# Transposing ctx of a second batch with VectorE's 32x32 blocks in an fp32 cross-attention and FFN kernel

## The reference, cut to what matters

```python
x = x + xattn(layernorm(x), ctx)      # x, ctx: (8, 256, 1024)
x = x + ffn(layernorm(x))             # 4-bit weights, 1024 x 1024

def xattn(text, features):
    Q = text @ Wq.T + bq
    K = features @ Wk.T + bk
    attn = softmax(Q @ K.T / sqrt(1024))
    return attn @ features
```

## Time and profile before

| | us |
|---|---|
| median of 3 runs | 547.48 |
| the profiled execution, its own time | 547.35 |
| its span, first to last instruction | 545.6 |
| TensorE busy | 539.3 (99%) |
| VectorE busy | 372.4 (68%) |
| ScalarE busy | 268.0 (49%) |
| GpSimd busy | 187.2 (34%) |

### The profile page before, as it was taken

One profiled execution on the slowest core, in us unless ns is written; L12 is line 12 of the kernel. 1 busy time (PEld: TensorE's weight loads), 2 busy tenths in 40 slices (PEclk: granted clock), 3 DMA queues, 4 the chain that ended last, 5 costly groups with the idle time before them and its releaser, 6 DMA issues.

```text
span 545.6 us, 7455 instructions
## 1 busy us (share of the span) xinstructions
PE 539.3 (99%) x2686; PEld 452.0 (83%) x2686; DVE 372.4 (68%) x616; ACT 268.0 (49%) x474; POOL 187.2 (34%) x147
## 2 busy tenths in 40 slices
PE   8999999999999999999999999999999999999997
PEld 7888888887777877778898999998788888888886
DVE  4989775787698774793424555574768779778742
ACT  6983444414767582343437766686563243324210
POOL 1072000010011000000326877777756644753530
PEclk9999999999999999999999999999999999999999
DMA  8942100359688756836384899898346775774311
GB/s 270 314 157 79 38 1 0 123 156 313 195 228 292 204 193 193 262 86 192 126 293 144 298 362 355 321 389 346 144 123 244 220 216 203 230 232 134 98 77 77
DMA packets 56036, 108.14 MB, mean 198 GB/s; under 512 B 12000, under 2 KB 32552, under 8 KB 53824
## 3 DMA queue, kind: packets, MB, share of 16 engines
q1 hardware_dynamic: 49472, 101.38, 54.1%
q10 hardware_dynamic: 6528, 6.29, 5.7%
HBM read 67.74 MB, written 39.85 MB: 197 GB/s over the span
## 4 chain that ended last, share of the span: by engine, by line
PE 86%; DVE 4%; ACT 3%; DMA 3%; issue 1%; POOL 1%; ACTq 0%; SPq 0%; DVEq 0%; POOLq 0%
PE bank L1337 22%; PE bank L1339 22%; PE bank L1338 22%; PE bank L1384 5%; PE bank L1390 5%; PE bank L1387 5%; PE bank L1438 2%; DMA xq<-xn_scratch 1%; ACT yin L868 1%; POOL cn_lo L578 1%; DVE xq L1035 1%; DMA wq_stage<-in_L_xattn_Wq 1%; DVE xT_lo L932 1%; PE bank L1347 1%; ACT cn_hi L627 1%
## 5 line engine op out<-in xcount | busy, mean ns | idle before, releaser
L1337 PE MATMUL bank<-xT_hi,m_hi 128*128 128x512 f32 x256 | 101.0, 395 | 0.0
L1339 PE MATMUL bank<-xT_hi,m_lo 128*128 128x512 f32 x256 | 99.7, 390 | 0.0
L1338 PE MATMUL bank<-xT_lo,m_hi 128*128 128x512 f32 x256 | 99.6, 389 | 0.0
L585 POOL TENSOR_TENSOR tT_lo<-t_pair,tT_hi 128x1024 fp32r<-128x1024 f32 x16 | 38.1, 2398 | 75.4 <-ACT tT_hi L627 75.4
L1289 DVE TENSOR_TENSOR xres<-xres,bank 128x512 f32<-128x512 f32 x56 | 38.3, 683 | 36.1 <-PE bank L1339 36.0
L599 POOL TENSOR_TENSOR l_lo_s<-l_sum_s,l_hi_s 128x512 fp32r<-128x512 f32 x32 | 40.4, 1297 | 56.0 <-DVE l_sum_s L1230 56.0
L824 ACT ACTIVATE t_pair<-bank,ucol 128x512 f32<-128x512 f32 x32 | 22.0, 687 | 74.1 <-PE bank L1339 69.6
L1337 PEld LDWEIGHTS bank<-xT_hi,m_hi 128*128 128x128 f32 x256 | 48.0, 188 | 11.8 <-issue 2.1
L1339 PEld LDWEIGHTS bank<-xT_hi,m_lo 128*128 128x128 f32 x256 | 48.0, 188 | 10.2
L1338 PEld LDWEIGHTS bank<-xT_lo,m_hi 128*128 128x128 f32 x256 | 48.1, 188 | 10.0 <-issue 0.2
L1384 PE MATMUL bank<-wk_hi,wq_hi 128*128 128x512 f32 x128 | 50.5, 394 | 0.2 <-DVE wq_lo L932 0.2
(11 more groups left out here) (158 smaller groups left out, 1244.0 us busy)
## 6 DMA issues: line engine op xcount, KB each, us to landing
xres<-in_x SPq DMA_DIRECT2D x8, 1024.0 KB, 11.9
out<-xres SPq DMA_DIRECT2D x15, 512.0 KB, 5.2
right_scratch<-part_hi SPq DMA_DIRECT2D x28, 256.0 KB, 2.2
cin<-in_ctx SPq DMA_DIRECT2D x7, 1024.0 KB, 6.1
xn_scratch<-xin SPq DMA_DIRECT2D x6, 1024.0 KB, 4.7
xq<-xn_scratch ACTq DMA_DIRECT2D x24, 256.0 KB, 5.4
r_tile<-right_scratch SPq DMA_DIRECT2D x6, 1024.0 KB, 12.2
yn_scratch<-yin SPq DMA_DIRECT2D x6, 1024.0 KB, 4.0
```

The lines of the kernel that those rows point to most:

```text
L585: pool.tensor_tensor(tT_lo[b][:, ks, :], t_pair[b // 2][:, b % 2, ks, :], tT_hi[b % 2 if b else 2][:, ks, :].bitcast(F32), ALU.subtract).t ...
L1337: pe.matmul(out_, a_hi, b_hi, start=start, stop=False, skip_group_check=True)
L1338: pe.matmul(out_, a_hi, b_lo, start=False, stop=False, skip_group_check=True)
L1339: return pe.matmul(out_, a_lo, b_hi, start=False, stop=stop, skip_group_check=True)
```

## The change

Batch 1 is treated as batch 0 was. Its quadrants are loaded into a second cq in the place where its natural rows were loaded, VectorE transposes them by blocks into banks 4 and 5 within the loop's b = 0, its splits u = 2 and 3 stand behind row_max(0), TensorE's c_tr(1, u) are gone, and its natural rows are loaded by four DMAs after the last of its blocks, ahead of load_x(0) in SyncE's order. Batches 2 to 7 stay with TensorE. The diff, cut to its core:

```diff
+BLOCKS = 2
-        cq = at("cq", 162.25, [P, NB, S], F32)
+        cq = [at(f"cq{b}", 162.25 + 8 * b, [P, NB, S], F32) for b in range(BLOCKS)]
...
         def ctx_loads(b):
-            return 16 * (b // 3 + 1) + (48 if b % 3 == 0 else 0)
+            return 16 * (b // 3 + 1) + (48 if b % 3 < BLOCKS else 0)
         def c_bank(b, u):
-            return bank[(3 if b else 6) + u % 2]
+            return bank[(6, 4, 3)[min(b, 2)] + u % 2]
...
-            def load_ctx(b):
+            def load_quadrants_of_ctx(b):
                 if b == 0:
-                    sp.wait_ge(s_cb, 4)
-                elif b == 1:
+                    sp.wait_ge(s_xlo, NB * PAIRS)
+                else:
                     for name in R_SUM:
                         sp.wait_ge(s_lst[name], 16 * KH)
+                pieces = ctx[b].rearrange("(j m) (k a i) -> a j (m k) i", m=NB, a=4, i=32)
+                for a in range(4):
+                    sp.dma_start(cq[b][32 * a:32 * a + 32, :, :].rearrange("p m (k i) -> p (m k) i", i=32),
+                                 pieces[a]).then_inc(s_cql[b], 16)
+
+            def load_ctx(b):
+                if b < BLOCKS:
+                    sp.wait_ge(s_cb, 4 * b + 4)
                 elif b == 2:
                     sp.wait_ge(s_t, NB * PAIRS)
                 else:
                     sp.wait_ge(s_cnlo, 4 * (b - 2))
-                    wait(sp, s_ctr, 4 * (b - 3))
-                if b == 0:
-                    rows = ctx[0].rearrange("(j t m) f -> m j t f", t=QT, m=4)
+                    wait(sp, s_ctr, 4 * (b - 4))
+                if b < BLOCKS:
+                    rows = ctx[b].rearrange("(j t m) f -> m j t f", t=QT, m=4)
                     for m in range(4):
-                        sp.dma_start(cin[0][32 * m:32 * m + 32, :, :], rows[m]).then_inc(s_cl[0], 16)
+                        sp.dma_start(cin[b][32 * m:32 * m + 32, :, :], rows[m]).then_inc(s_cl[b], 16)
...
-            load_ctx(1)
+            load_quadrants_of_ctx(1)
             load_ctx(0)
...
             load_ctx(2)
             load_right(0, 0, 3)
+            load_ctx(1)
...
             def c_hi(b, u):
-                if b == 0:
-                    act.wait_ge(s_cb, u + 1)
-                else:
-                    act.wait_ge(s_ctr, 4 * (b - 1) + u + 1)
+                if b < BLOCKS:
+                    act.wait_ge(s_cb, 4 * b + u + 1)
+                else:
+                    act.wait_ge(s_ctr, 4 * (b - BLOCKS) + u + 1)
+                if b == 1:
+                    act.wait_ge(s_t, NB * PAIRS)
...
-            def c_blocks(u):
+            def c_blocks(b, u):
                 if u == 0:
-                    dve.wait_ge(s_cql, 64)
+                    dve.wait_ge(s_cql[b], 64)
+                    if b == 1:
+                        dve.wait_ge(s_w, 4 * KH)
                 if u > 1:
-                    dve.wait_ge(s_clo, u - 1)
+                    dve.wait_ge(s_clo, 4 * b + u - 1)
...
             for b in range(B):
...
-                if b + 1 < B:
+                if b == 0:
+                    c_blocks(1, 0)
+                    c_blocks(1, 1)
+                    c_lo(1, 0)
+                    c_blocks(1, 2)
+                    c_lo(1, 1)
+                    c_blocks(1, 3)
+                elif b + 1 < B:
                     c_lo(b + 1, 0)
                     c_lo(b + 1, 1)
...
                 row_max(b)
+                if b == 0:
+                    c_lo(1, 2)
+                    c_lo(1, 3)
...
                     if j in (3, 7):
-                        if b + 1 < B:
+                        if BLOCKS <= b + 1 < B:
                             c_tr(b + 1, j // 2 - 1)
                             c_tr(b + 1, j // 2)
-                        else:
+                        elif b + 1 == B:
                             y_tr(0, ("a21", "a22") if j == 3 else ("a11", "a12"))
```

More of the change, by code:

```diff
@@ L232, in xattn_ffn_kernel @@
         s_cl = [sem(f"ctx_loaded{i}") for i in range(3)]
-        s_cql, s_cb = sem("ctx_by_quadrant_loaded"), sem("ctx_transposed_by_blocks")
+        s_cql = [sem(f"ctx{b}_by_quadrant_loaded") for b in range(BLOCKS)]
+        s_cb = sem("ctx_transposed_by_blocks")
         s_ctr, s_chi, s_clo = sem("ctx_transposed"), sem("cT_hi_done"), sem("cT_lo_done")
@@ L455, in _ @@
                     if n == NB * (PAIRS - 1) + 1:
[L456 to L460, removed]
+                        load_quadrants_of_ctx(0)
                     for k, i in HI_AT.get(n, ()):
@@ L855, in y_apply @@
                     act.wait_ge(s_cnlo, 4 * (B - 2))
-                    act.wait_ge(s_ctr, 4 * (B - 3))
+                    act.wait_ge(s_ctr, 4 * (B - 4))
                 elif f == 1:
@@ L1135, in right_lo @@
                 low(part_lo[k][name], part[k][name], part_hi[(N_PROD * k + i) % 2], s_rlo)
-            def c_blocks(u):
+            def c_blocks(b, u):
                 if u == 0:
-                    dve.wait_ge(s_cql, 64)
+                    dve.wait_ge(s_cql[b], 64)
+                    if b == 1:
+                        dve.wait_ge(s_w, 4 * KH)
                 if u > 1:
-                    dve.wait_ge(s_clo, u - 1)
-                dve.transpose(c_bank(0, u)[:, :].rearrange("p (k m j) -> p m k j", k=2, m=NB),
-                              cq.rearrange("p m (k i) -> p m k i", i=32)[:, :, 2 * u:2 * u + 2, :]).then_inc(s_cb, 1)
+                    dve.wait_ge(s_clo, 4 * b + u - 1)
+                dve.transpose(c_bank(b, u)[:, :].rearrange("p (k m j) -> p m k j", k=2, m=NB),
+                              cq[b].rearrange("p m (k i) -> p m k i", i=32)[:, :, 2 * u:2 * u + 2, :]).then_inc(s_cb, 1)
             def c_lo(b, u):
@@ L1179, in _ @@
                     if p == PAIRS - 1 and j == 5:
-                        c_blocks(0)
-                        c_blocks(1)
+                        c_blocks(0, 0)
+                        c_blocks(0, 1)
                     if p == PAIRS - 1 and j == 6:
                         c_lo(0, 0)
-                        c_blocks(2)
+                        c_blocks(0, 2)
                         c_lo(0, 1)
-                        c_blocks(3)
+                        c_blocks(0, 3)
             c_lo(0, 2)
@@ L1431, in c_tr @@
                     pe.wait_ge(s_cl[b % 3], ctx_loads(b))
-                if b == 1 and u == 0:
+                if b == BLOCKS and u == 0:
                     pe.wait_ge(s_tev, NB * PAIRS)
```

## The result

The changed kernel takes 551.34 us in the median of 9 runs (548.97 to 553.39), the kernel before 547.63 us in 9 runs (547.1 to 548.25): a ratio of 1.0067, 95% interval 1.0054 to 1.008. It is 3.7 us **slower**; forecast were 546.2 us and a range up to 547.8. The times also spread over 4.4 us, where those of before spread over 1.2. The profiled execution took 550.0 us, its span is 548.2 us.

A forecast was written before the change was run, and what follows sets the result against it. TensorE's own work and a chain from VectorE's row_max(0) to pv(0) were taken to bound the stretch. 2.1 us earlier less a 0.8 us stall for xres(0) made 1.3 us less: 546.2 us, range 545.0 to 547.8.

The forecast's parts named there:

- the one under the loads: SyncE's queue at pv(0)'s fourth group: xres(0), issued at 289.2, lands at 298.0, so TensorE stalls 0.8 us.
- the sum: Landing times of queued loads in order: batch 2 286.9, r_tile 290.7, batch 1's rows 294.8, xres(0) 297.3 at the earliest.
- The price of the pieces: Natural rows loaded in four pieces: move at 258 GB/s, 4.1 us for a MB, against 2.5 us for whole loads.
- rival 4: xres(0) behind SyncE's wait takes 11.9 us, lands at 301.1, pv(0)'s fourth group stalls 3.9 us: 549.3 us, chance 0.07.
- TensorE's 1.74 us: Batch 1's sixteen transposes leave TensorE, two groups of 0.87 us, so scores(1) starts at 285.3 instead of 287.08.
- the two waits that vanish: TensorE's idling before pv(0): 0.44 us before 294.70 and 0.2 us inside a transpose group; all gone, gain 2.4 us.
- the quadrants, hidden: Load of batch 1's quadrants: lands at 280.3, 2.2 us before VectorE asks, so it costs nothing.
- the tight splits: VectorE's two splits moved behind row_max(0) end at 288.6, with little room before batch 2's transposes; costed at nothing.
- tT_lo at no cost: GpSimd's tT_lo(1,0) ends at 285.13, just ready for scores(1) at 285.3: costs nothing.
- the 2.1 us of the forecast: VectorE's row_max(0) starts at 286.7 instead of 288.85, moving the chain through pv(0) 2.1 us earlier.
- Rival 3: VectorE's chain late, by slower block transposes or late quadrants: 547.1 or 547.3 us; 548.7 if blocks lie bare; chance 0.10.
- the rule on transposes: Use TensorE for 128x128 transposes when the result may go to PSUM; would make the swap lose 1.2 us, 548.7.

The follow-up runs named there:

- e1: Changed kernel with the load of xres(0) issued ahead of the four loads of batch 1's natural rows: 545.67 us against 547.51 before, ratio 0.997.
- e7: Changed kernel with batch 1's natural rows in one 1 MB load instead of four pieces (batch 1's attention then not the reference's): 545.27 us in one run.
- e9: Changed kernel, unchanged, profiled a third time: 551.64 us.
- e4: Kernel before the change, with its load of xres(0) held until p_lo(0) is done: 549.13 us against 547.51, ratio 1.0037.
- e5: e1 with the first 1.5 MB of r_tile issued behind the load of batch 3's ctx: 545.62 us against 547.70 before, ratio 0.9962.
- e6: Changed kernel with SyncE holding batch 3's ctx, the r_tile chunk and xres(1) until xres(0) has landed: 549.32 us against 547.70 before, ratio 1.0034.

## Why the prediction was wrong

**The step that failed** is the one under the loads: "Lower bound of its landing: 297.3 ... Upper: ... 299.8 ... I take 298.0 ... a stall of 0.8 us". The mechanism was right (SyncE's wait for the last block, four issues, xres(0) at 289.2, residual(0,0), bank 5), and so was the moment from which it hurts; the landing was 300.4, 300.5 and 301.2 in three executions, the stall 2.7 to 4.0 us. Less the 0.57 us by which the first of these executions was late, its landing is 299.9: the stated upper bound of 299.8 was reached once and passed twice. Up to batch 2's load the sum nearly held, 287.5 (288.1 less 0.57) against 286.9. Then it parts: r_tile landed at 293.1 instead of 290.7, the last of batch 1's pieces at 297.5 instead of 294.8. Three things were taken wrongly in it; how the microseconds divide among them is not shown.
- *In order.* The sum let each load have the engines alone, in the order of issue. The first piece of batch 1's rows landed at 293.0, ahead of r_tile at 293.7, which was issued 6 us earlier; in e1 the first piece landed at 295.5, ahead of xres(0) at 296.7, which was issued a microsecond earlier. The Trainium skill ("DMA: Bandwidth & Descriptors", section on queues, rings and completion order) says that a copy is split over up to 16 of its queue's rings, and that completion does not follow the order of issue of an engine. The traces agree, by these numbers.
- *The price of the pieces.* 4.1 us for a MB came from the best stretch of batch 0's rows, 258 GB/s; behind a backlog the queues moved 209 to 229 for 6 us, pieces and the rest of r_tile together. At that rate a MB takes 4.6 to 5.0 us, and r_tile's rest was slowed with it, which the sum had at 414. With the MB in one load (e7) the queues moved 401.
- *The choice of the row.* I had a row for such a load in the thick of the loop, 11.9 us in the median, and gave it 0.07 as rival 4; the three landings took 10.7 to 12.0 us. The load that I took as nearest, 7.0 us, had a single load of 1.5 MB ahead of it.

**The clock had no term.** A wait of TensorE was priced at its own length. The granted clock fell behind the longer waits, and the stretch behind them took 1.5 us more in the profiled execution (5.68 - 4.14) and 2.4 us more in e9 (6.58 - 4.14), of which some 0.2 is the start after a wait, as in e4. The account for the profiled execution: 2.3 earlier, 2.66 waiting with 0.2 before it for the last product to end, 1.5 in the stretch behind it, 0.57 of lateness from the stages before, makes 2.6 us more, which is the spans' 548.2 - 545.6.

**Right** were: TensorE's 1.74 us and the two waits that vanish (c_tr(2,2) came 2.3 us earlier, by the distance from batch 2's load: 14.60 us before, 12.33 after); the blocks' 0.71 us; row_max(0), at 287.10 with 0.57 of shift in it, so 286.5 against 286.7; the quadrants, hidden (VectorE waited for nothing there); the tight splits and tT_lo at no cost. By e1 and e5 the swap is worth 1.8 to 2.1 us, the 2.1 us of the forecast, once the load is out of its way. Rival 3, late blocks, was wrong, and with it what the rule on transposes (the Trainium skill, "VectorE: DVE Perf Modes", rules for kernel authors) would make of this place: VectorE could take them because it had idle time (68% busy) and TensorE (99%) had not.

## What to carry to other kernels

When a step is moved to a less busy engine, the loads that follow it move too. Look on the issuing queue for what stands behind the new wait, and price its landing with the thickest traffic in the trace, not the thinnest, and not as if loads landed in order. A load that is wanted soon belongs ahead of one that is wanted later; e1 and e5 show it here. And look at the granted clock behind a new wait of TensorE: here 2.7 us of waiting brought 1.5 us more behind it, nearly all of it slow products.

## What the runs showed that I had not expected

TensorE's granted clock stayed full behind waits of 1.44 (e6) and 1.90 us (e4) and was down to 1.2 GHz behind waits of 2.66, 2.98, 3.32 and 3.98 us, in kernels with and without the change; what happens between 1.90 and 2.66 us is not shown. The products behind those waits took 0.63 us instead of 0.40 in the trace, at a pace of 0.43 instead of 0.23 us each, until 2.9 to 4.9 us after the restart: 1.5 to 1.7 us were lost behind the three shorter waits and 2.4 us behind the longest. So a load whose landing differs by 1.3 us between three executions moved the place behind it by 2.2 us (14.37 to 16.58 from the transposes before pv(0) to those of batch 3).
